# Three bank pairs and a half-image stagger in the per-image head of a Fourier tower

## The reference, cut to what matters

```python
x = coords @ fc0_w + fc0_b
for sw, cw, cb in layers:                       # four layers
    x = gelu(spectral_conv(x, sw) + pointwise(x, cw) + cb)
x = gelu(x @ fc1_w + fc1_b)                     # 32 -> 64, the head's first layer
h = (x @ fc2_w + fc2_b)[..., 0]                 # 64 -> 1, the head's second layer
h = concat([cls_tok, h])                        # 65 tokens of 64 for each image
h = h + attention(layernorm(h)) ; h = h + experts(layernorm(h))
```

## Time and profile before

| what | value |
|---|---|
| median of 3 runs | 1084.4 us (1083.52 to 1084.65) |
| the profiled execution's own time | 1083.5 us |
| its span, first to last instruction | 1081.6 us |
| mean granted TensorE clock, as a share of full speed | 0.973 |
| busy share of the span: PE, PEld | 91%, 58% |
| busy share of the span: DVE, ACT, POOL | 57%, 37%, 14% |
| head 1, first matmul to the start of the last addition | 369.48 to 421.00 us |
| head 2, first matmul to the start of the tail's first matmul | 763.34 to 810.77 us |

### The profile page before, as it was taken

The page is one execution under the profiler, slowest core; times in us unless marked ns, Lnnn a source line. Parts: engine busy times, 40 slices in busy tenths (PEclk is TensorE's granted clock), DMA queues, the critical chain, the costliest instruction groups (busy, mean ns, idle before and its releaser), DMA issues.

```text
span 1081.6 us, 36566 instructions
## 1 busy us (share of the span) xinstructions
PE 979.3 (91%) x17004; PEld 623.9 (58%) x17004; DVE 617.2 (57%) x773; ACT 397.9 (37%) x522; POOL 151.4 (14%) x158
## 2 busy tenths in 40 slices
PE   4899899999989999999899899999899898688885
PEld 3667667657656533676567567656216687533342
DVE  2268457737833221587278357633143677769887
ACT  2432233224223486232332233224675567411100
POOL 6000000000000000000000000020010765334421
PEclk9999999999999899999999999999999899779998
DMA  5220230032022201310220220030001000000000
GB/s 196 93 78 3 69 90 17 3 105 67 4 90 102 59 6 40 109 30 3 93 78 4 78 87 9 4 100 10 14 14 44 2 2 1 2 1 1 2 11 10
DMA packets 25918, 46.78 MB, mean 43 GB/s; under 512 B 9949, under 2 KB 11000, under 8 KB 25125
## 3 DMA queue, kind: packets, MB, share of 16 engines
q1 hardware_dynamic: 24118, 42.47, 12.5%
q0 software_dynamic: 1456, 1.63, 0.6%
q10 hardware_dynamic: 192, 0.33, 0.1%
HBM read 30.25 MB, written 10.89 MB: 38 GB/s over the span
## 4 chain that ended last, share of the span: by engine, by line
PE 74%; DVE 12%; issue 5%; ACT 3%; POOL 3%; DMA 2%; SPq 1%; POOLq 0%; DVEq 0%
PE PSALL L1296 22%; PE PSALL L1264 7%; PE PSALL L1158 5%; PE PSALL L1287 5%; PE PSALL L1373 5%; PE PSALL L1239 4%; PE PSALL L1172 4%; PE PSALL L526 3%; PE PSALL L1383 3%; DVE WORK L1503 3%; PE PSALL L427 2%; DVE WORK L1003 2%; PE PSALL L513 2%; DVE WORK L1522 2%; PE PSALL L1135 2%
## 5 line engine op out<-in xcount | busy, mean ns | idle before, releaser
L1522 DVE STREAM_TRANSPOSE WORK<-PSALL 128x1024 f32<-128x1024 f32 x128 | 152.5, 1230 | 252.9 <-PE PSALL L1264 252.9
L1296 PEld LDWEIGHTS PSALL<-EW,WORK 128*64 128x64 f32 x4096 | 221.8, 138 | 72.8 <-issue 48.3
L1296 PE MATMUL PSALL<-EW,WORK 128*64 128x128 f32 x4096 | 247.6, 276 | 14.0 <-DVE WORK L1522 13.7
L1422 ACT ACTIVATE X<-PSALL,TABLES 128x1024 f32<-128x1024 f32 x128 | 141.8, 1114 | 307.2 <-PE PSALL L1296 307.2
L1503 DVE STREAM_TRANSPOSE WORK<-PSALL 128x1024 f32<-128x1024 f32 x84 | 104.3, 1242 | 32.8 <-PE PSALL L1158 30.9
L324 POOL DMA_DIRECT2D WORK<-MIXED x32 | 17.6, 550 | 670.5 <-ACT MIXED L1413 557.2
L1404 ACT COPY SPEC<-PSALL 128x400 f32<-128x400 f32 x64 | 54.4, 850 | 136.6 <-PE PSALL L1172 132.9
L1172 PEld LDWEIGHTS PSALL<-TABLES,WORK 128*64 128x64 f32 x2000 | 67.1, 138 | 48.8 <-DVE WORK L1503 31.4
L1003 DVE TENSOR_TENSOR WORK<-PSALL,X 128x832 f32<-128x832 f32 x80 | 79.3, 1017 | 16.8 <-PE PSALL L513 15.3
L1172 PE MATMUL PSALL<-TABLES,WORK 128*64 128x64 f32 x2000 | 80.7, 228 | 7.9 <-DVE WORK L1503 3.8
L1456 ACT ACTIVATE WORK<-PSALL,B 128x1024 f32<-128x1024 f32 x64 | 67.8, 1110 | 19.7 <-PE PSALL L1373 19.4
(11 more groups left out here) (157 smaller groups left out, 1157.7 us busy)
## 6 DMA issues: line engine op xcount, KB each, us to landing
SW<-in_spec_w SPq DMA_DIRECT2D x160, 80.0 KB, 2.8
spec_scr<-MIXED SPq DMA_DIRECT2D x24, 400.0 KB, 3.3
SPEC<-spec_scr SPq DMA_DIRECT2D x32, 200.0 KB
WORK<-spec_scr SPq DMA_DIRECT2D x16, 200.0 KB
WORK<-in_coords_w SPq DMA_DIRECT2D x2, 1024.0 KB, 4.8
XC<-in_coords_c SPq DMA_DIRECT2D x2, 1024.0 KB, 7.2
WORK<-MIXED SPq DMA_DIRECT2D x40, 40.0 KB
WORK<-MIXED POOLq DMA_DIRECT2D x32, 40.0 KB
```

Of the source, the lines that this page charges most:

```text
L1296: m = pe.matmul(PS[2 * p + z][64 * j:64 * j + 64, 2 * b * GRID:(2 * b + 2) * GRID], G[:, n % 2, b, h:h + 2, :, t].rearrange("p q o -> p (q ...
L1422: nc.scalar.activation(X[:, n].rearrange("p b (z d) c w -> p d z b (c w)", z=2)[:, p, :, :, 2 * t * GRID:2 * (t + 1) * GRID], PSALL[:, 2 * ...
L1522: nc.vector.transpose(G[:, n % 2, 2 * x + y].rearrange("p h o v -> p o h v"), PSALL[:, 4 + 2 * x:6 + 2 * x, :].rearrange("p k (h o v) -> p ...
```

## The change

Each image's first layer now goes into three pairs of banks in turn, (2, 3), (4, 5) and (6, 7): half k uses `head_pair(k)`. Before the loop the first half of image 0 is issued. Step m0 then issues the second half of image m0 together with the first half of image m0 + 1, as eight matmuls with j outermost and the four row groups inside it (`head_first`), behind one wait for both gelus of image m0 - 1. The second layer of image m0 - 1 comes after them as before; it uses banks 0 and 1 in turn in the last pass, and bank 0 alone in pass 0. There, bank 1 serves the pointwise weights, the rows of the coordinates and all expansions, so each expansion waits for the copy of the one before, and `first_rows(0)` waits for VectorE to have copied the pointwise weights, which it now does before image 0. The counts of matmuls, gelus, copies, additions and DMAs stay what they were.

```diff
@@ -35,6 +35,16 @@
 PIXELS_IN_INVERSE = [[], [], [], [2], [3], [0, 1], [4, 5], [6, 7, 8, 9, 10, 11]]
 PIXELS_AFTER = [[], [12], [], [], [13], [], [], [14], [], [], [15], [], [], [], [], []]
 PIXEL_ORDER = [k for slot in PIXELS_IN_INVERSE + PIXELS_AFTER for k in slot]
+
+
+def head_pair(k):
+
+    return (2, 4, 6)[k % 3]
+
+
+def head_banks(p):
+
+    return 2 if p == PASSES - 1 else 1
 
 
 def pair_of(k):
@@ -1198,27 +1208,30 @@
                 firsts.wait(xw_in, 1)
                 dft_columns(PS[4:8], [COORDS[:, i] for i in range(NOCT)]).then_inc(c0_full.sem, 1)
 
-            def first_pointwise():
+            def first_pointwise(bank):
                 for i in range(OCT):
                     for p in range(4):
-                        m = pe.matmul(PS[3][Q * p:Q * p + Q, i * CH:(i + 1) * CH], F0[:, i, :], TABLES[0:CH, 0, 0:CH],
+                        m = pe.matmul(PS[bank][Q * p:Q * p + Q, i * CH:(i + 1) * CH], F0[:, i, :], TABLES[0:CH, 0, 0:CH],
                                       start=True, stop=True, tile_position=(0, Q * p))
                 m.then_inc(w0_full.sem, 1)
 
-            def first_rows(s):
+            def first_rows(s, bank):
                 firsts.wait(z0_ready, s + 1)
-                m = dft_rows(0, PS[2], s * SPW, ZC[:, s])
+                m = dft_rows(0, PS[bank], s * SPW, ZC[:, s])
                 if s == NOCT - 1:
                     m.then_inc(s0_full.sem, 1)
 
-            def first_expand(r):
+            def first_expand(r, banks):
                 if r == 0:
                     firsts.wait(s0_ready, 1)
                     firsts.wait(w0_ready, 1)
-                if r >= 2:
-                    turn.wait(sp_ready, r - 1)
+                if banks is spec_bank:
+                    if r >= 2:
+                        turn.wait(sp_ready, r - 1)
+                elif r:
+                    turn.wait(sp_ready, r)
                 for i in range(2 * r, 2 * r + 2):
-                    m = pe.matmul(PS[2 + r % 2][:, i % 2 * SPW:(i % 2 + 1) * SPW], E0[:, i % OCT, :],
+                    m = pe.matmul(banks[r % 2][:, i % 2 * SPW:(i % 2 + 1) * SPW], E0[:, i % OCT, :],
                                   S0[:, i // OCT * SPW:(i // OCT + 1) * SPW], start=True, stop=True)
                 m.then_inc(sp_full.sem, 1)
                 if r == ROUNDS - 1:
@@ -1346,12 +1359,23 @@
                         if n + 1 < NG:
                             inverse_rows(l, n + 1, t)
 
+            def head_first(p, tiles):
+
+                for j in range(2):
+                    for image, d in tiles:
+                        if image < GIMG:
+                            m = pe.matmul(PS[head_pair(2 * image + d // 2) + d % 2][FC * j:FC * (j + 1), :], W1[Q * d:Q * d + Q, :],
+                                          X[Q * d:Q * d + Q, image // B4, image % B4, 2 * j:2 * j + 2].rearrange("p q c w -> p (q c w)"),
+                                          start=True, stop=True, tile_position=(Q * d, FC * j))
+                            if j and d % 2:
+                                m.then_inc(fc1_full.sem, 1)
+
             first_columns_dft()
-            first_pointwise()
+            first_pointwise(3)
             for s in range(NOCT):
-                first_rows(s)
+                first_rows(s, 2)
             for r in range(ROUNDS):
-                first_expand(r)
+                first_expand(r, spec_bank)
             for p in range(PASSES):
                 layer(p, 0)
                 turn.next()
@@ -1361,35 +1385,31 @@
 
                 turn.wait(x_ready, 0)
                 turn.wait(g_ready, 0)
+                head_first(p, [(0, 0), (0, 1)])
                 for m0 in range(GIMG + 1):
+                    if m0:
+                        passes.wait(fc1_ready, 2 * m0)
                     if m0 < GIMG:
-                        for d in range(4):
-                            k = 2 * m0 + d // 2
-                            if d == 0 and m0 == 0 and p + 1 < PASSES:
-                                firsts.wait(z0_ready, NOCT)
-                            if d % 2 == 0 and k >= 2:
-                                passes.wait(fc1_ready, k - 1)
-                            for j in range(2):
-                                m = pe.matmul(PS[4 + d][FC * j:FC * (j + 1), :], W1[Q * d:Q * d + Q, :],
-                                              X[Q * d:Q * d + Q, m0 // B4, m0 % B4, 2 * j:2 * j + 2].rearrange("p q c w -> p (q c w)"),
-                                              start=True, stop=True, tile_position=(Q * d, FC * j))
-                            if d % 2:
-                                m.then_inc(fc1_full.sem, 1)
+                        if m0 == 0 and p + 1 < PASSES:
+                            firsts.wait(z0_ready, NOCT)
+                        head_first(p, [(m0, 2), (m0 + 1, 0), (m0, 3), (m0 + 1, 1)])
                     if m0:
-                        if m0 >= 3:
-                            passes.wait(fc2_ready, m0 - 2)
-                        passes.wait(fc1_ready, 2 * m0)
+                        banks = head_banks(p)
+                        if m0 > banks:
+                            passes.wait(fc2_ready, m0 - banks)
                         for i in range(FB):
-                            m = pe.matmul(PS[(m0 - 1) % 2][32 * i:32 * i + 32, :], W2[:], FH[:, (m0 - 1) % 2 * FB + i, :],
+                            m = pe.matmul(PS[(m0 - 1) % banks][32 * i:32 * i + 32, :], W2[:], FH[:, (m0 - 1) % 2 * FB + i, :],
                                           start=True, stop=True, tile_position=(0, 32 * i))
                         m.then_inc(fc2_full.sem, 1)
                     if p + 1 < PASSES:
                         if m0 == 0:
-                            first_pointwise()
+                            first_pointwise(1)
                         if m0 in (1, 2):
-                            first_rows(m0 - 1)
+                            if m0 == 1:
+                                firsts.wait(w0_ready, 1)
+                            first_rows(m0 - 1, 1)
                         if EXPAND_AT <= m0 < EXPAND_AT + ROUNDS:
-                            first_expand(m0 - EXPAND_AT)
+                            first_expand(m0 - EXPAND_AT, [PS[1], PS[1]])
                 passes.wait(fc2_ready, GIMG)
                 passes.next()
             tail_tensor(pe)
@@ -1424,9 +1444,9 @@
                     PSALL[:, 2 * p:2 * p + 2, :].rearrange("p z (b n) -> p z b n", b=B4),
                     ACT.Gelu, bias=TABLES[:, l, BIAS:BIAS + 1]).then_inc(x_ready.sem, 1)
 
-            def first_spectrum():
+            def first_spectrum(bank):
                 firsts.wait(s0_full, 1)
-                nc.scalar.copy(S0[:], PS[2][:, 0:NOCT * SPW]).then_inc(s0_ready.sem, 1)
+                nc.scalar.copy(S0[:], PS[bank][:, 0:NOCT * SPW]).then_inc(s0_ready.sem, 1)
                 firsts.next()
 
             def layer(p, l):
@@ -1439,7 +1459,7 @@
                         for d in range(2):
                             activated(l, n, t, d)
 
-            first_spectrum()
+            first_spectrum(2)
             for r in range(ROUNDS):
                 spectrum(r, spec_bank)
             for p in range(PASSES):
@@ -1453,13 +1473,13 @@
                         if m >= 2 and e == 0:
                             passes.wait(fc2_full, m - 1)
                         s = k % 4 * 2
-                        nc.scalar.activation(FH[:, s:s + 2, :], PSALL[:, 4 + 2 * e:6 + 2 * e, :], ACT.Gelu, bias=B1[:, 0:1]
+                        nc.scalar.activation(FH[:, s:s + 2, :], PSALL[:, head_pair(k):head_pair(k) + 2, :], ACT.Gelu, bias=B1[:, 0:1]
                                              ).then_inc(fc1_ready.sem, 1)
                     if p + 1 < PASSES:
                         if m == 2:
-                            first_spectrum()
+                            first_spectrum(1)
                         if EXPAND_AT <= m < EXPAND_AT + ROUNDS:
-                            spectrum(m - EXPAND_AT, spec_bank)
+                            spectrum(m - EXPAND_AT, [PS[1], PS[1]])
                 passes.next()
             tail_scalar(act)
 
@@ -1509,9 +1529,9 @@
                 for s in range(NOCT):
                     rows_onto_partitions(ZC[:, s], 4, s).then_inc(z0_ready.sem, 1)
 
-            def first_weights():
+            def first_weights(bank):
                 firsts.wait(w0_full, 1)
-                nc.vector.tensor_copy(W0[:].rearrange("p a b -> p (a b)"), PS[3][:, 0:OCT * CH]).then_inc(w0_ready.sem, 1)
+                nc.vector.tensor_copy(W0[:].rearrange("p a b -> p (a b)"), PS[bank][:, 0:OCT * CH]).then_inc(w0_ready.sem, 1)
                 firsts.next()
 
             def inverse_rows_out(n, y, x):
@@ -1546,7 +1566,7 @@
 
             in_head, tail = tail_vector(dve)
             first_rows_onto_partitions()
-            first_weights()
+            first_weights(3)
             for p in range(PASSES):
                 layer(0)
                 turn.next()
```

(6 more changed lines are left out.)

## The result

The changed kernel takes 1074.66 us (median of 4 runs, 1073.5 to 1077.76) where the kernel before takes 1084.53 (4 runs beside them, 1083.52 to 1085.12). The ratio is 0.9935, with a 95% interval of 0.9909 to 0.9961: faster. Forecast were 1080.9 and a range of 1077.5 to 1082.9.

The account below looks back on a forecast made before the run. TensorE, fed by halves, was taken to bound head 2, with TensorE and ScalarE both near the pace in head 1. Head 2's -3.6 and head 1's +0.1 gave -3.5 us, median 1080.9, range 1077.5 to 1082.9.

Parts of the forecast that it names:

- the mechanism in head 2: Steady head 2: issuing the eight first-layer matmuls together cuts an image from 2.67 to 2.35 us, a gain of 0.32.
- Eight matmuls in the new order: First layer in the heads: a set of eight takes 1.04 us, with 1.15 and 2.0 as the ends.
- The loop of head 2: Steady head 2: gelu end, next eight matmuls, then the gelu on their last half, 2.35 us per image against 2.67.
- The end of head 2: From image 7's addition VectorE's own chain through the stores sets the pace; image 15 comes 3.6 us earlier.
- the load of the centre: End of head 2: issued when the store lands, it lands 3.3 us later, at 804.8, just before the centre at 804.87.
- In head 1 the end: Last addition comes 10.18 us after image 11's, against 9.75 before, because second layer and addition alternate in one bank.
- The sum, -3.6 + 0.1: Whole kernel: head 2 3.6 us faster plus head 1 0.1 slower, -3.5 us in all.
- The clock at the starts of the heads: Rival: TensorE's half-clock stretches in one or both heads go, 1.5 to 4 us lower, say 1078.3; chance 0.22.
- The point against it: Heads' start: argument against the half-clock stretches going, that the idle 1.2 us ahead of image 0's second gelu stays.
- the copy on ScalarE: Head 1, expansions: ScalarE's copy takes 0.91 us, read from 396.51 to 397.42, beside two gelus at 1.01.
- head 1's steps: Head 1 with expansions: 3.05 us per image, two taking 6.10 against 6.21, a gain of 0.4 over eight images.
- the steps of images 5 and 9: Head 1, behind a store: these images wait 0.2 us each for the second layer's single bank.

Follow-up runs that it names:

- e1: Kernel before with two extra matmuls per head, results unread, keeping TensorE busy at the heads' starts: 1077.6 us against 1080.97, ratio 0.9959.
- e4: Changed kernel with one more wait per head, so the first eight matmuls wait for the gelu of image 0's first half: 1083.61 us, ratio 1.0011 to the kernel before.
- e7: The changed kernel again, no edit, beside the kernel before on one chip in five rounds: 1074.15 us against 1082.94, ratio 0.9938.
- the larger comparisons: Two reruns of the unedited changed kernel against the kernel before: 1074.15 us against 1082.94 (ratio 0.9938) and 1074.88 against 1083.06 (0.9939).
- e8: Changed kernel with a single bank for the second layer in head 2 too: 1084.57 us, ratio 1.002 to the kernel before.
- e2: New order in head 2 alone, head 1 keeping its old code, banks and waits: 1075.9 us, ratio 0.9943 to the kernel before.

## Why the prediction was wrong

**At full clock the mechanism in head 2 was right, step by step.** Eight matmuls in the new order take 1.05 to the next start (forecast 1.04). The loop of head 2 is 2.37 (2.35). The end of head 2 is VectorE's: 45.83 in e1 against 42.37 is 3.5 us (3.6), and the load of the centre still fits, landing 3.1 after its issue (3.3). The tail follows. In head 1 the end is 10.32 long (10.18); the steps ahead of it were mis-sized, as told below.

**The step that failed is the treatment of the clock.** The sum, -3.6 + 0.1, has no term for it: the forecast took it as a thing that would stay as it was, and kept the other case as a rival ("The clock at the starts of the heads") with a chance of 0.22. That rival came true. In all three profiles of the changed kernel both heads have 1.00, in the profile before 0.93 and 0.96. e1 priced the clock at 2.6 in head 1 and 1.6 in head 2, 4.2 together, just above the rival's 1.5 to 4; e4 took the gain away by putting one idle time back. The evidence was in the earlier trace rows and in the starts of the heads, where the longer first burst stood in the diff; I had written both down and given the case a fifth of the chance. The point against it, that an idle time of over a microsecond stays ahead of the work on image 1, was true in head 2 (1.38 us) and did not decide. The forecast also compared one profiled execution with a median, while the kernel before varies between 1078.66 us, with a mean granted clock of 0.978, and 1085.88, with 0.970, on one chip.

**Two terms of head 1 that were mis-sized**: the copy on ScalarE, 0.91, was a start-to-start distance that ended in a wait, and is 0.64. With it head 1's steps are 2.91 instead of 3.05. Against that, the steps of images 5 and 9 are 0.5 longer and not 0.2. At full clock head 1 gains 0.4 to 0.6 (49.72 or 49.75 to 49.12 to 49.31), where I had 0.1 lost. (The opening also calls ScalarE's work per image the longest in the steady head. By its own figures it is 2.02 there, beside TensorE's 2.04; nothing rests on it.)

**What is not in the heads**: of the first comparison's 9.6 us, 2.25 lie in the layers of pass 1. The kernel before had a stretch at half clock there (0.51 from 699.3 to 702.8 us), and e7, the changed kernel, had one too (0.51 from 511.4 to 514.8), with 341.2 us for the same layers. So this part need not be the change's own, and the larger comparisons, with 8.8 and 8.2 us between the medians where the heads explain 8.3, do not need it. Why these layers and the tail (270.6 to 276.0) sometimes take longer, at a slightly lower mean clock, was not tried.

With the clock's 4.2 (2.6 + 1.6) and the copy's part taken in, the sum would have been about 8 us, 1076. The 1.5 us from there to 1074.66 are fewer than the 2.25 in the layers, which are that one execution's.

## What to carry to other kernels

When TensorE waits in short bursts, look for a granted clock below 1.00 in those stretches, and price a new order twice: by its own chain at full clock, and by the idle it removes or leaves. Test the clock's share by filling the idle with matmuls that nobody reads, in the old kernel, before crediting the order with it. A start-to-start distance is the cost of an instruction only if nothing that the next one waits for arrived inside it.

## What the runs showed of the hardware

- Two idle times of 1.21 and 1.33 us around a burst of 1.09 stood ahead of a granted clock of 1.2 GHz (e4), and one idle time of 2.25 ahead of the one that lasted to the end of the head (e8). It is not certain each time: the old head 1 had idle times of 1.2 and 0.52 around its first burst both where the clock fell (the kernel before) and where it did not (e2). The Trainium skill (TensorE: Matmul & The Clock Gate, "HAM oscillation") tells of a kernel whose waits between bursts throttle the engine again and again, and has its loop restructured so that the engine stays warm. The traces agree, and show it with waits shorter than the DMA waits of that kernel.
- Eight fp32 matmuls of 32 rows, 64 columns and 512 pixels on eight different tiles run in 1.12 us whichever of the two orders of row group and column tile is issued; the same eight take 2.02 at half clock.
- Four extra matmuls, 1.13 us each in the trace of e1, made the old kernel 3.4 us faster (1080.97 to 1077.6).
